# A transformer block with two routed expert layers on one core: router weights held stationary in four column groups, and the attention's side work given out to other steps and engines

## The reference

```python
x = x + 0.5 * ffn(layernorm(x))      # routed experts, first time
x = x + attn(layernorm(x))           # 16 heads of 16, RMS norm and rotation of q and k
x = x + 0.5 * ffn(layernorm(x))      # the same routed experts again
# ffn: logits = x @ w_switch + b_switch          (256 -> 8 experts)
#      each token goes to its best expert, in token order, up to a capacity of 512
#      h = relu(buf_e @ w1 + b1); y = h @ w2 + b2   (256 -> 1024 -> 256 per expert)
#      tokens over the capacity pass through; the output has the shape of x
# attn: softmax(q k' / 4 + 1) v, then @ wproj.T
```

## Time and profile before

| | |
|---|---|
| runs | 2403.99 us median, 2403.72 to 2404.91 |
| the profiled execution, its own time | 2410.09 us |
| its span | 2408.2 us |
| first maximum of attention | 443.96 us |
| last tile's maximum | 2073.8 us |
| second experts from | 2207.7 us |
| mean granted TensorE clock | 0.964 of 2.4 GHz |

### The profile page before, as it was taken

How to read it: one execution, slowest core, us unless ns; L and a number is a source line. 1 busy time by engine, 2 the same in 40 slices (tenths; PEclk the granted TensorE clock), 3 DMA queues, 4 the chain that set the end, 5 groups by cost and what they waited for, 6 DMA issues and landing times.

```text
span 2408.2 us, 36923 instructions
## 1 busy us (share of the span) xinstructions
PE 2194.1 (91%) x13224; PEld 1160.7 (48%) x13224; DVE 1735.6 (72%) x2555; ACT 1731.4 (72%) x3390; POOL 977.8 (41%) x1157
## 2 busy tenths in 40 slices
PE   6759974699899999999999999999999999996997
PEld 6738963343344434434444343444444334344896
DVE  5637755578788888798888779878887988413674
ACT  5846654358788788788878878887887887844663
POOL 3764423163273256239226623922751101113442
PEclk9999996599899999999999999999999999998998
DMA  5734331513344334334433434443343334101431
GB/s 201 261 100 172 137 105 49 91 28 82 80 81 109 57 82 101 73 58 108 98 59 86 90 76 60 98 96 59 76 106 58 68 59 107 49 17 63 158 106 62
DMA packets 144904, 218.33 MB, mean 91 GB/s; under 512 B 32225, under 2 KB 100955, under 8 KB 144465
## 3 DMA queue, kind: packets, MB, share of 16 engines
q1 hardware_dynamic: 135504, 199.01, 34.6%
q0 software_dynamic: 9216, 16.95, 2.0%
...
## 4 chain that ended last, share of the span: by engine, by line
PE 74%; DVE 10%; POOL 5%; issue 4%; ACT 4%; DMA 2%; SPq 1%; POOLq 0%; DVEq 0%; ACTq 0%
PE PS L800 18%; PE PS L784 17%; PE PS L767 10%; DVE NMX L1352 5%; PE PS L712 5%; PE PS L584 4%; PE PS L744 3%; PE PS L683 2%; PE PS L681 2%; PE PS L682 2%; POOL buf L1477 2%; PE PS L665 2%; PE PS L667 2%; PE PS L666 2%; PE PS L616 2%
## 5 line engine op out<-in xcount | busy, mean ns | idle before, releaser
L1352 DVE TENSOR_REDUCE NMX<-PS 128x1 f32<-128x1024 f32 x1024 | 1224.2, 1219 | 293.1 <-PE PS L767 287.7
L1043 ACT ACTIVATE PB<-PS 128x512 f32<-128x512 f32 x2048 | 1105.2, 605 | 229.6 <-PE PS L784 222.0
L784 PE MATMUL PS<-QF,KF 51*128 51x512 f32 x2048 | 802.9, 462 | 15.4 <-DMA QF<-MT 7.7
L767 PE MATMUL PS<-KF,QF 49*128 49x512 f32 x2048 | 727.5, 450 | 40.8 <-DVE NMX L1352 25.0
L784 PEld LDWEIGHTS PS<-QF,KF 51*128 51x128 f32 x2048 | 330.2, 185 | 558.2 <-ACT PB L1043 280.5
L800 PE MATMUL PS<-PB,V 128*17 128x512 f32 x4096 | 543.0, 602 | 0.2
L767 PEld LDWEIGHTS PS<-KF,QF 49*128 49x128 f32 x2048 | 317.6, 189 | 173.3 <-DVE NMX L1352 107.3
L1458 POOL TENSOR_TENSOR RS<-VE,NEGH 128x8 f32<-128x8 f32 x24 | 40.2, 1676 | 373.9 <-DVE VE L1148 373.9
L1279 DVE TENSOR_TENSOR HLR<-HL,HHR 128x512 fp32r<-128x512 f32 x128 | 88.6, 693 | 88.2 <-ACT HHR L973 88.2
L1569 POOL TENSOR_TENSOR R1R<-R,HI 128x512 fp32r<-128x512 f32 x56 | 71.7, 1282 | 183.1 <-ACT R L1010 183.1
L681 PE MATMUL PS<-W2H,HLR 128*128 128x256 f32 x512 | 143.1, 279 | 0.0
...
## 6 DMA issues: line engine op xcount, KB each, us to landing
...
```

The lines of the kernel that those rows point to most:

```text
L767: m = e.matmul(PS[:, 2 * i + half, :], QF[k][at:at + ROWS_S, p * SEQ + ti * 128:p * SEQ + ti * 128 + 128], KF[k][at:at + ROWS_S, p * SEQ + ...
L784: e.matmul(PS[:, bank, :], KF[k][at:at + ROWS_ST, p * SEQ + sbk * 128:p * SEQ + sbk * 128 + 128], QF[k][at:at + ROWS_ST, p * SEQ + th * 51 ...
L1043: e.activation(PB[j % 3][:, h * 512:(h + 1) * 512], PS[:, place["e", tile], :], ACT.Exp).then_inc(e_out, 1)
L1352: e.tensor_reduce(NMX[:, u % 2, at:at + 1], PS[:, 2 * i:2 * i + 2, :], AX.XY, ALU.max, negate=True).then_inc(s_max, 1)
```

## The change

The router. WSW is widened to 32 columns (24 of them zero, set by POOL at the start) and is the stationary operand; the transposed rows move, 256 columns of them. The four groups of a batch go to four column groups of the array, so eight matmuls make all logits, as 8 rows in each quarter of one PSUM bank. ACT copies the bank to LT (one copy of 128x256), PE transposes LT in two matmuls, and DVE adds the bias straight from PSUM. Logits thus wait for all four transposed groups. XTQ is gone; in the first routing odd batches use a second XTP.

The side work. All tables are new (below). A batch's preparation starts 24 steps ahead and not 12 (batches 1, 2 and 3 at steps 4, 57 and 110). q and k tiles come every third step and not every second. Of the scaling of the first four tiles (hf 0) and of the low parts of their pieces, POOL's share for batches 1 to 7 goes to DVE; POOL keeps the other four. QK has three buffers, not two. `rope_out` and `sp_lo` become a semaphore for each half. The second routing's later parts (from `shift` on) come 12 steps or more later, and the last step of the tail goes from NS+77 to NS+95.

Batch 0. DVE rotates all eight tiles and then scales all eight; before, it scaled the first four between the fourth and the fifth. Pieces are cut in another order (PIECES_0): first the four that units 0 and 1 need, then, in steps 0 to 4 of attention, the other four, whose low parts POOL makes. `load_unit` of units 0 and 1 waits for the stores of four pieces. The load of PX for batch 1 comes in step 1, not ahead of step 0.

```diff
-EARLY = 12
-XT_AT = (9, 10, 11, 12)
-QK_AT = (16, 18, 20, 22, 24, 26, 28, 30)
-ROOT_AT = (24, 32)
-SPLIT_AT = ((29, 31, 37, 39), (41, 43, 45, 47))
-VALUES_AT = (53, 55, 57, 59)
-FIRST_SPLIT = 4
+EARLY = 24
+XT_AT = (12, 13, 14, 15)
+QK_AT = (17, 20, 23, 26, 29, 32, 35, 38)
+ROOT_AT = (27, 39)
+SCALE_AT = (31, 33, 34, 36)
+VALUES_AT = (47, 50, 52, 54)
+PIECES = ((37, 0, 0), (39, 0, 1), (40, 0, 2), (42, 0, 3), (45, 1, 0), (46, 1, 1), (48, 1, 2), (49, 1, 3))
+PIECES_0 = ((40, 0, 0), (41, 0, 2), (42, 1, 0), (43, 1, 2), (0, 1, 1), (1, 1, 3), (2, 0, 1), (4, 0, 3))
+BEGIN = {1: 4, 2: 57, 3: 110, **{b: BATCH * (b - 1) - EARLY for b in range(4, 8)}}
...
-LATER = Way(inverse=LEAVE, ..., transposes=[LEAVE + t for t in (3, 4, 6, 8)],
-            logits=[LEAVE + t for t in (5, 7, 9, 10)], shift=LEAVE + 11, exp=LEAVE + 12, softmax=(LEAVE + 13, LEAVE + 14),
-            settle=[LEAVE + 22 + i // 2 for i in range(8)], scatter=[LEAVE + 26 + i for i in range(8)])
-LAST = LEAVE + 34
+LATER = Way(inverse=LEAVE, ..., transposes=[LEAVE + 3 + g for g in range(4)],
+            logits=LEAVE + 7, back=LEAVE + 22, shift=LEAVE + 23, exp=LEAVE + 24, softmax=(LEAVE + 25, LEAVE + 26),
+            settle=[LEAVE + 36 + i // 2 for i in range(8)], scatter=[LEAVE + 43 + i for i in range(8)])
+LAST = LEAVE + 52
-AGAIN_AT = {**{n: 7 for n in range(13, 16)}, 16: 2, 17: 6, 18: 2, 19: 6, 20: 1, 21: 4}
+AGAIN_AT = {17: 7, 18: 7, 19: 7, 20: 5}
...
 def load_px(b):
     if b:
-        e.wait_ge(sp_full, 8 * b)
+        e.wait_ge(sp_full, 8 * b if b > 1 else 6)
 def load_unit(u):
-        e.wait_ge(st_q[i], 128 * (b + 1))
+        e.wait_ge(st_q[i], 64 if u < 2 else 128 * (b + 1))
...
 def route(c):                      # PE
-    for g in range(4):
-        yield way.logits[g]
-        e.wait_ge(xtq_out, 4 * c + g + 1)
-        for i in range(2):
-            for ch in range(2):
-                m = e.matmul(PS[:, bank, i * 8:i * 8 + 8], xtq(c, g)[:, ch, i * 128:(i + 1) * 128],
-                             WSW[:, ch, :], start=(ch == 0), stop=(ch == 1))
+    yield way.logits
+    e.wait_ge(xtq_out, 4 * c + 4)
+    for ch in range(2):
+        for g in range(4):
+            m = e.matmul(PS[32 * g:32 * g + 32, bank, 0:256], WSW[:, ch, :], xtq(c, g)[:, ch, :],
+                         start=(ch == 0), stop=(ch == 1))
+    yield way.back
+    e.wait_ge(lg_out, c + 1)
+    transposes(bank, [LT[:, j * 128:(j + 1) * 128] for j in range(2)]).then_inc(lt_full, 1)
...
 def pre_x(b):                      # DVE
-        if kk == 3 and b == 0:
-            yield ROOT_AT[hf] + 1
-            e.wait_ge(rq_root, hf + 1)
-            for i in range(4):
-                scale(e, n - 3 + i)
+        if b:
+            for i in range(4):
+                if QK_AT[t] < SCALE_AT[i] <= (QK_AT + (99,))[t + 1]:
+                    yield SCALE_AT[i]
+                    e.wait_ge(rq_root, 2 * b + 1)
+                    scale(e, 8 * b + i)
+    if b == 0:
+        yield ROOT_AT[1] + 1
+        for hf in range(2):
+            e.wait_ge(rq_root, hf + 1)
+            for i in range(4):
+                scale(e, 4 * hf + i)
 def split(b, first=0, count=8):    # DVE; POOL has the other condition
+    for k, at, hf, j, m in pieces(b, first, count):
+        if hf == 0 and b or k < 4 and b == 0:
+            yield at + 1
+            e.tensor_tensor(LO[:, k % 2, :], R1[:, k % 2, :], HI[:, k % 2, :].bitcast(F32), ALU.subtract)
```

More of the change, by code:

```diff
@@ L59 @@
+BEGIN = {1: 4, 2: 57, 3: 110, **{b: BATCH * (b - 1) - EARLY for b in range(4, 8)}}
 PROJ_AT = (32, 33, 34, 35, 36, 37, 38, 39)
-Way = namedtuple("Way", "inverse normal transposes logits shift exp softmax onehot own count slots settle scatter")
+Way = namedtuple("Way", "inverse normal transposes logits back shift exp softmax onehot own count slots settle scatter")
 FIRST = Way(inverse=2, normal=[5 + i // 2 for i in range(8)], transposes=[7 + g for g in range(4)],
-            logits=[9 + g for g in range(4)], shift=14, exp=16, softmax=(17, 17), onehot=(18, 18),
+            logits=11, back=13, shift=14, exp=16, softmax=(17, 17), onehot=(18, 18),
@@ L71 @@
-LAST = LEAVE + 34
+LATER = Way(inverse=LEAVE, normal=[LEAVE + 1 + i // 2 for i in range(8)], transposes=[LEAVE + 3 + g for g in range(4)],
+            logits=LEAVE + 7, back=LEAVE + 22, shift=LEAVE + 23, exp=LEAVE + 24, softmax=(LEAVE + 25, LEAVE + 26),
+            onehot=(LEAVE + 27, LEAVE + 28), own=LEAVE + 29, count=LEAVE + 30,
+            slots=(LEAVE + 31, LEAVE + 32, LEAVE + 33, LEAVE + 34, LEAVE + 35),
+            settle=[LEAVE + 36 + i // 2 for i in range(8)], scatter=[LEAVE + 43 + i for i in range(8)])
@@ L116, in run, with values_at, pieces, prepare @@
         self.live = [s for s in self.live if s[1] is not None]
-def split_at(b, hf, j):
-    return SPLIT_AT[hf][j] + (FIRST_SPLIT if b == 1 else 0)
-def prepare(side, n, b, pre_x, *parts):
+def values_at(b, g):
+    return VALUES_AT[g] - (4 if b == 2 else 0) if b else BATCH - 5 + g
+def pieces(b, first=0, count=8):
+    table = PIECES if b else PIECES_0
+    for k in range(first, first + count):
+        at, hf, j = table[k]
+        yield k, at, hf, j, sum(p[1] == hf for p in table[:k])
+def prepare(side, n, b, pre_x, split, values=None):
     side.begin(n, pre_x(b))
-    for part in parts:
+    side.begin(n, split(b) if b else split(b, 0, 4))
+    if values is not None:
         for g in range(4):
-            side.begin(n, part(b, g))
+            side.begin(n, values(b, g))
 def build_program(nc, NB, x_in, wqkv, wproj, gq, wsw, bsw, w1, b1, w2, b2, cst, out):
@@ L549, in sync_program @@
                 if n == 0:
-                    side.begin(0, before(1))
-                if r == BATCH - EARLY - 3 and b + 2 < NB:
-                    side.begin(n + 3, before(b + 2))
+                    side.begin(n, stores(0, 4, 4))
+                    side.begin(BEGIN[1], before(1))
+                for k in range(2, NB):
+                    if n == BEGIN[k] - 3:
+                        side.begin(n + 3, before(k))
                 if r == 0 and 1 <= b <= NB:
@@ L714, in projected, with split @@
                 return m
-            def split(b, j):
-                for hf in range(2):
-                    yield split_at(b, hf, j)
-                    n = 8 * b + 4 * hf + j
-                    e.wait_ge(rope_out, 8 * b + 4 * hf + 4)
-                    bank = ring("split", n)
+            def split(b, first=0, count=8):
+                for k, at, hf, j, m in pieces(b, first, count):
+                    yield at
+                    e.wait_ge(rope_out[hf], 4 * b + 4)
+                    bank = ring("split", 8 * b + k)
                     take(bank)
                     transposes(bank, [QR[:, 4 * hf + i, j * 128:(j + 1) * 128] for i in range(4)]).then_inc(sp_full, 1)
-                    busy[bank] = (sp_raw, n + 1)
+                    busy[bank] = (sp_raw, 8 * b + k + 1)
             def values(b, g):
-                yield VALUES_AT[g]
+                yield values_at(b, g)
                 e.wait_ge(xt_lo, 4 * b + g + 1)
@@ L999, in pre_x, with split @@
                     e.activation(SQ[:, :], PS[:, bank, :], ACT.Square).then_inc(qk_sq, 1)
-            def split(b, j):
-                for hf in range(2):
-                    n = 8 * b + 4 * hf + j
-                    yield split_at(b, hf, j)
+            def split(b, first=0, count=8):
+                for k, at, hf, j, m in pieces(b, first, count):
+                    n = 8 * b + k
+                    yield at
                     e.wait_ge(sp_full, n + 1)
@@ L1431, in turn @@
             if n >= 8:
[L1433 removed]
+                e.wait_ge(sp_full, 8 * (n // 8) - (4 if t < 4 and n >= 16 else 0))
             if own.n:
```

187 lines of the change are left out of this document (98 added, 89 removed).

## The result

| | before | changed |
|---|---|---|
| median of six runs on one chip | 2404.45 us | 2420.1 us |
| lowest and highest | 2399.73, 2408.08 | 2416.73, 2429.36 |
| the profiled execution, its own time | 2410.09 | 2425.95 |
| span | 2408.2 | 2424.1 |
| first maximum of attention | 443.96 | 425.49 |

The ratio of changed to before is 1.0072 (95% interval 1.0051 to 1.0093). The forecast was 2381 us (2356 to 2400): wrong in sign. Attention starts 18.5 us earlier, as forecast, and takes 31.6 us longer. Its batches took 206.5, 207.0, 207.2, 207.2, 211.5, 207.2, 203.3 us; now 195.3, 213.4, 220.5, 215.3, 215.3, 218.0, 205.7. Batch 0 is 11.2 us shorter, batches 1 to 6 are 44.8 us longer.

What follows compares the result with a forecast made beforehand. The prediction took PE, busy 91% of the span, to set the pace, with DVE and ACT close behind. Its terms summed to -23.1 us, taking the profiled 2410.09 to 2387, or 2381 us in the runs (range 2356 to 2400).

Steps and rivals of the forecast that it cites:

- First routing: Before attention: shorter router logits on PE start POOL's inverse roots earlier; -4.5 us, bounds 0 and -7.
- rival C: Router logits: column groups don't overlap in the short matmuls and run one by one; 2402 us, chance 0.06.
- Preparation: Batch 0 before attention: reordered scaling and pieces bring the first unit's load earlier; -14.6 us, bounds -10 and -17.
- Stall at step 52: Batch 0: PE's wait for unit 2's maxima, and the clock's fall after it, go; -11 us, bounds 0 and -12.
- Logits in attention: Second routing on PE: shorter logits gain 1.75 us a batch, seven times; -12 us.
- Crowding: Attention: moved side work on DVE and ACT costs 3.5 us in each of four batches; +14 us.
- (c): Crowding in steps 15 to 18: ACT needs some 15.3 us where PE needs 12.0; +3 us a batch.
- The waits added: Attention, step 7: DVE waits for the root, just in time, with maxima and scores behind it; no separate size.
- (a): Crowding in steps 40 to 44: moments of PX fall on those of QX; +4.5 us a batch.
- D: Rival: DVE's burst in steps 3 to 13 waits for the root, crowding over 6 us a batch; 2415 us, chance 0.12.
- A: Rival: no crowding in attention, neighbouring steps average everywhere; 2367 us, chance 0.18.
- B: Rival: the next batch's unit comes late, PE waits at step 64, the clock falls; 2389 us, chance 0.12.

Runs made afterwards that it cites:

- e16: e6 with batch 2's preparation begun at step 56 and not 52: 2369.3 us, 0.9853 of the kernel before.
- e15: e6 run once more, unchanged, as the parent on the same chip: 2379.9 us, 0.9895 of the kernel before.
- e6: Kernel before plus only the new router and batch 0's order; attention's side-work tables, store steps and POOL's share as before: 2378.7 us, 0.9898.
- e1: Changed kernel with a batch's last four pieces cut at steps 45, 47, 49, 51, not 45, 46, 48, 49: 2407.2 us, 1.0011 of the kernel before.
- e2: Changed kernel with settle's eight instructions spread one a step over eight steps, not two a step over four: 2412.3 us, 1.0028 of the kernel before.
- e7: e6 with the first four scalings and low parts on DVE, scalings at 27 to 30, first pieces at 31 and 33: 2387.6 us, 0.9924.
- e8: Changed kernel with pieces of batches 2 to 7 two steps apart, v projections and DVE's scalings moved, settle one a step: 2394.9 us, 0.9966.

## Why the prediction was wrong

- **First routing** (-4.5, bounds 0 and -7): POOL's inverse root starts at 38.34 and not 44.46, and the first row of the experts' scaling at 151.81 and not 158.88: -7.1, just past the bound. The 16 records of 256 columns take 1.07 us, so the column groups overlap and rival C falls:

```profile
20.14 1.07 PE L641 MATMUL PS<-XTP,WSW 128*32 128x256 f32 x16 [0.86 <-ACT XTP L945]
```

- **Preparation** (-14.6, bounds -10 and -17): -18.5 less 7.1 is -11.4. The first transfer goes at 410.75, the first maximum comes at 425.49, against the earlier trace rows. Right mechanism, within bounds.
- **Steps 0 to 19 of batch 0** (+6 with the tiles' later cost): 57.62 us against 60.69, so -3; steps 20 to 49, with the tiles that were moved out, take 2.8 more. Together about 0, the lower bound.
- **Stall at step 52** (-11): gone; steps 50 to 55 of batch 0 fall from 30.4 to 20.6 us, -9.8. In the other tables of e16 and e15 its going is worth 13.1 in batch 0.
- **Logits in attention** (-1.75 a batch): PE's starts advance by 1.00 us for the logits and 0.37 for LT's transposes, 3.88 before; the batch falls from 207.2 to 205.7 in e6, so -1.5. The Trainium skill has a change of tiling mode drain the array (TensorEngine Tiling (Array Packing), Key Properties); no run here separates a drain from the 1.00 us, which is about what an L800 group takes to the next start (0.99) with such changes on both sides. Over seven batches -1.5 is -10.5, near the -12.
- **Tail** (-1): +2.7; with the tables of before it is -3.4 (e6, 329.4 from last maximum to end), as the later routing steps reach further behind attention.
- **Crowding** (+14, four batches at 3.5) is the step that failed. Against e6, batches 1 to 6 are 58 us longer: 44 more than the term, where the whole forecast is 39 too low. I summed work per engine and spread it; that sum saw (c) settle with HI and R1 right, 15.3 us of ACT where PE needs 12.0, and priced it at +3 less what neighbours take up. The four steps took 15.96, the fall of the clock included. "The waits added" named DVE's wait for the root alone. It does not occur in the changed kernel: in step 7 DVE is busy 4.17 of 4.20 us. The wait that does occur, HI for a store that the table issues in the same step, is nowhere in it, though the earlier trace rows has HI waiting 23.0 us for that DMA and the table's steps give the collision by subtraction. Nor is the store that stands behind a unit's load in SP's queue (PE idle 4.45 us in batch 2, against my sign of no idle time over 2 us). Nor is a fall of the clock behind any new wait, though I had priced one at 4.8 us for step 52. e1 and e2 are worth 13 and 8 of it, DVE's share 9 (e7, in its own setting). The other 28 were not split edit by edit. But e8, which does the same work and only loosens its steps, takes back 37.5 of the 49.8 us that batches 2 to 6 of the changed kernel are above e6's; of the 12.3 left the share alone would make 7.5. So most of the loss is waits and the clock behind them, and some 5 us stay open.
- **(a) Steps 40 to 44** (+4.5 less relief): 17.77 us, and 13.5 in batch 6, which has no moments of PX; the price was about right.
- **Rivals.** D gave 2415 and 0.12, and the time was near it, with half its mechanism: crowding over 6.2 a batch, yes (9.6 in the mean), DVE's wait for the root, no: that its number was near is luck. A's 2367 without crowding is near the 2369 of e16, which has the tables of before. B did not occur. C's own sum was off (2.75 a batch in seven batches is 19, not 16), which changes nothing.
- **L1489**: the mean of 1630 ns was read as the time beside DVE's subtractions. 12 of the 56 take 2.7 us (those beside subtractions all along), the others 1.2 to 1.6, some at 1.22 with over 0.8 us of subtractions beside them. No term hung on it.
